# Gate and routing of a gated cross-attention and mixture-of-experts layer: searches in the logits, softmax and tables on GpSimd, more fillers on TensorE

## The reference, cut to what matters

```python
def _L0_ffn_ref(x, gate_w, w1, b1, w2, b2):
    gate_logits = jnp.einsum('bsh,eh->bse', x, gate_w)
    gate_probs = jax.nn.softmax(gate_logits, axis=-1)
    top_v, top_i = jax.lax.top_k(gate_probs, TOP_K)
    onehot = jax.nn.one_hot(top_i, E, dtype=x.dtype)
    comb_w = jnp.einsum('bsk,bske->bse', top_v, onehot)
    out = jnp.zeros_like(x)
    for e in range(E):
        h = jax.nn.silu(jnp.einsum('bsh,hf->bsf', x, w1[e]) + b1[e])
        y = jnp.einsum('bsf,fh->bsh', h, w2[e]) + b2[e]
        out = out + y * comb_w[..., e:e + 1]
    return out
x = x + jnp.tanh(g_xattn[0]) * _L0_xattn_ref(_layernorm(x), ctx_1024, itok, Wq, Wkv, Wo)
x = x + jnp.tanh(g_ffn[0]) * _L0_ffn_ref(_layernorm(x), gate_w, w1, b1, w2, b2)
```

## Time and profile before

| | us |
|---|---|
| runs | 357.92, 358.46, 357.48 (median 357.92) |
| profiled execution, its own time | 356.72 |
| its span, first to last instruction | 355.0 |
| busy: PE / DVE / POOL / ACT | 325.0 / 269.9 / 206.1 / 174.1 |
| mean granted clock of TensorE | 0.976 |

### The profile page before, as it was taken

The page is one execution under the profiler, slowest core; times in us unless marked ns, Lnnn a source line. Parts: engine busy times, 40 slices in busy tenths (PEclk is TensorE's granted clock), DMA queues, the critical chain, the costliest instruction groups (busy, mean ns, idle before and its releaser), DMA issues.

```text
span 355.0 us, 11408 instructions
## 1 busy us (share of the span) xinstructions
PE 325.0 (92%) x3466; PEld 268.6 (76%) x3466; DVE 269.9 (76%) x638; ACT 174.1 (49%) x490; POOL 206.1 (58%) x223
## 2 busy tenths in 40 slices
PE   6798999999989889999999999999999999999930
PEld 6557878888789678888888888888888887778710
DVE  4479999999977987778877788787887875665520
ACT  2451355565464456656465565654656543253400
POOL 3486889996752071566647757467573864662330
PEclk9999999999996999999999999999999999999995
DMA  7699999998999421132323323232332323242210
GB/s 251 201 343 416 408 416 403 416 404 325 347 384 394 113 64 34 32 60 37 52 41 63 46 48 48 47 63 40 55 47 49 51 44 62 36 65 26 35 18 13
DMA packets 31406, 53.23 MB, mean 150 GB/s; under 512 B 4834, under 2 KB 25554, under 8 KB 29300
## 3 DMA queue, kind: packets, MB, share of 16 engines
q0 software_dynamic: 9408, 26.63, 29.3%
q1 hardware_dynamic: 15972, 22.44, 17.4%
q10 hardware_dynamic: 5968, 3.39, 3.2%
HBM read 42.29 MB, written 10.17 MB: 148 GB/s over the span
## 4 chain that ended last, share of the span: by engine, by line
PE 64%; DVE 21%; issue 4%; DMA 4%; ACT 2%; POOL 2%; DVEq 0%; ACTq 0%; POOLq 0%
PE ps L1082 29%; PE ps L1096 16%; PE ps L1099 8%; DVE ps L1262 5%; DVE sel L1258 3%; PE ps L1110 2%; PE ps L1104 2%; DVE w_parts L1258 2%; DMA sel<-near_rows,win_near 2%; DMA tokens_split<-xsplit 1%; DVE xs L1294 1%; PE ps L1103 1%; PE ps L1098 1%; PE ps L837 1%; DVE ps L1266 1%
## 5 line engine op out<-in xcount | busy, mean ns | idle before, releaser
L1082 PE MATMUL ps<-sel,w_parts 128*128 128x128 f16 x1776 | 141.3, 219 | 0.9 <-issue 0.9
L1082 PEld LDWEIGHTS ps<-sel,w_parts 128*128 x1776 | 119.4, 98 | 25.7 <-issue 1.4
L816 ACT ACTIVATE sel<-ps,b1T 128x128 f32<-128x128 f32 x296 | 84.3, 368 | 91.2 <-PE ps L1082 90.7
L589 POOL DMA_INDIRECT out<-sel x37 | 63.2, 1707 | 85.2 <-DVE sel L1532 73.2
L1096 PE MATMUL ps<-w_parts,sel 128*128 x259 | 96.4, 379 | 0.4
L1099 PE MATMUL ps<-w_parts,sel 128*128 x259 | 70.6, 273 | 0.0
L581 POOL DMA_INDIRECT sel<-tokens_split,sel x37 | 45.1, 1219 | 19.2 <-DVE sel L1455 12.7
L1487 DVE SCALAR_TENSOR_TENSOR sel<-sel 128x512 f16<-128x512 f32 x74 | 51.3, 693 | 2.5
L1473 DVE SCALAR_TENSOR_TENSOR w_parts<-w_parts (+1 forms) x32 | 39.0, 1220 | 8.4 <-issue 6.9
L1485 DVE TENSOR_SCALAR sel<-sel 128x512 f16<-128x512 f32 x74 | 33.6, 454 | 9.9 <-ACT sel L816 9.5
L576 POOL TENSOR_TENSOR sel<-sel 128x1 f32<-128x1 f32 x37 | 38.6, 1043 | 1.9 <-PE ps L1110 1.9
(11 more groups left out here) (221 smaller groups left out, 466.6 us busy)
## 6 DMA issues: line engine op xcount, KB each, us to landing
w_parts<-in_L_ffn_w SPq DMA_DIRECT2D x16, 1024.0 KB
out<-xs SPq DMA_DIRECT2D x16, 128.0 KB
tokens_split<-xsplit ACTq DMA_DIRECT2D x16, 128.0 KB, 5.7
xs<-in_x ACTq DMA_DIRECT2D x2, 512.0 KB, 7.0
near_rows<-w_parts SPq DMA_DIRECT2D x4, 256.0 KB, 6.2
xs<-in_x SPq DMA_DIRECT2D x2, 512.0 KB
sel<-tokens_split,sel POOLq DMA_INDIRECT x37
out<-sel POOLq DMA_INDIRECT x37
```

The costliest lines, as they stand in the source:

```text
L589: pool.indirect_dma_start(out_rows, bass.IndirectOffsetOnAxis(slot_row[:, at(q - 1)], 0), y_sb[(k + 3) % 4], None, compute_op=ALU.add).the ...
L816: act.activation(h32[n][:, c * P:c * P + P], ps_h[n][:, c * P:c * P + P], ACT.Silu, bias=biases[:, c:c + 1], scale=1.0 / (X_SCALE * W_SCALE))\
L1082: mm = pe.matmul(ps_h[n][:, c * P:c * P + P], w, xx, start=(i == 0), stop=(i == len(products) - 1))
```

## The change

The two searches run in the logits and no longer in the probabilities, now in a part of 11 tiles and one of 5. The softmax's subtraction goes to POOL, in one instruction for 16 tiles, its exponential is one instruction on ACT, its sum and reciprocal stay on DVE after the running sum, and the weights are multiplied on POOL in three instructions. POOL also takes the experts' order (13 instructions instead of DVE's 3), the small tables (4 instead of 3) and the two products by the token's number. All of these stand in POOL's program behind the last norms; the clearing of `b2_wide` and the gathers stand behind them. PE has more fillers between the last logits (10, 10, 12, 8 where 4, 4, 8, 4 stood) and fewer after them (36 for 48).

```diff
@@ POOL
             norms(T - 1, 1)
+            pool.wait_ge(s["rt"], RT_TOP)
+            pool.tensor_tensor(r_tmp[:, :, :], logit[:, :, :], r_m8[:, :, 0:1].to_broadcast([P, T, E]), ALU.subtract)\
+                .then_inc(s["shifts_ok"], 1)
             remainder(T - 2)
             remainder(T - 1)
+            pool.wait_ge(s["rt_exp"], 1)
+            pool.tensor_scalar(r_p[:, :, :], r_ex[:, :, :], gate2[:, 0:1], None, ALU.mult).then_inc(s["comb_ok"], 1)
+            pool.wait_ge(s["rt"], RT_CUM)
+            pool.wait_ge(s["comb_ok"], 1)
+            pool.tensor_tensor(r_p[:, :, :], r_p[:, :, :], r_m16[:, :, :], ALU.mult).then_inc(s["comb_ok"], 1)
+            pool.wait_ge(s["rt"], RT_INVERSE)
+            pool.wait_ge(s["comb_ok"], 2)
+            pool.tensor_tensor(r_comb[:, :, :], r_p[:, :, :], <r_rs over experts>, ALU.mult).then_inc(s["comb_ok"], 2)
+            pool.wait_ge(s["rt"], RT_RANK)
+            for r in range(E):
+                ins = pool.tensor_scalar(r_by[:, r, :], r_rank[:, :], float(r), None, ALU.is_equal)
+            ins.then_inc(s["ordering"], 1)
...
+            pool.tensor_copy(order_i[:, 1:E + 1], order_f[:, :]).then_inc(s["ordered"], 1)
+            pool.wait_ge(s["span_ok"], 1)
+            pool.tensor_scalar(e_new[:, :], iota[0:E, 0:NT], e_col[:, 0:1], None, ALU.is_equal).then_inc(s["tables"], 1)
+            pool.tensor_scalar(e_ended[:, :], iota[0:E, 0:NT], e_col[:, 1:2], None, ALU.is_ge).then_inc(s["tables"], 1)
+            pool.tensor_scalar(e_own[:, :], iota[0:E, 0:NT], e_col[:, 0:1], None, ALU.is_ge).then_inc(s["tables"], 1)
+            pool.wait_ge(s["tables"], 3)
+            pool.tensor_tensor(e_own[:, :], e_own[:, :], e_ended[:, :], ALU.subtract).then_inc(s["tables"], 1)
+            for h in range(2):
+                tokens = slice(T // 2 * h, T // 2 * h + T // 2)
+                pool.wait_ge(s["rt"], RT_HOT + 1 + h)
+                pool.tensor_tensor(col_tok[:, tokens, :, :], col_tok[:, tokens, :, :], spread_pairs(tok16[:, :], NT),
+                                   ALU.mult).then_inc(s["tok_ok"], 1)
             pool.wait_ge(s["o_ps"], T)
             pool.memset(b2_wide, 0.0).then_inc(s["b2_zeroed"], 1)
@@ ACT
-            act.wait_ge(s["rt"], RT_SHIFT)
-            act.activation(r_ex[:, 0:LATE, :], r_tmp[:, 0:LATE, :], ACT.Exp).then_inc(s["rt_exp"], 1)
...
-            act.wait_ge(s["rt"], RT_SHIFT_LATE)
-            act.activation(r_ex[:, LATE:T, :], r_tmp[:, LATE:T, :], ACT.Exp).then_inc(s["rt_exp"], 1)
+            act.wait_ge(s["shifts_ok"], 1)
+            act.activation(r_ex[:, :, :], r_tmp[:, :, :], ACT.Exp).then_inc(s["rt_exp"], 1)
...
-            act.wait_ge(s["rt"], RT_COMB)
+            act.wait_ge(s["comb_ok"], 4)
...
-            act.wait_ge(s["rt"], RT_ORDER)
+            act.wait_ge(s["ordered"], 1)
@@ PE
             second_turn(T - 3)
-            spin(4)
+            spin(10)
             logits(T - 3)
             second_turn(T - 2)
-            spin(4)
+            spin(10)
             logits(T - 2)
+            spin(12)
+            second_turn(T - 1)
             spin(8)
-            second_turn(T - 1)
-            spin(4)
             logits(T - 1)
-            spin(48)
+            spin(36)
             pe.wait_ge(s["rt"], RT_CUM)
...
             pe.wait_ge(s["rt"], RT_ROWS)
+            pe.wait_ge(s["tok_ok"], 1)
             rows_into_list(0, 8)
...
             pe.wait_ge(s["rt"], RT_ROWS + 2)
+            pe.wait_ge(s["tok_ok"], 2)
             rows_into_list(16, 24)
@@ DVE
-            def shifted_logits(some):
+            def top_two(some):
                 dve.wait_ge(s["logit_ok"], some.stop)
-                link(v.tensor_reduce(r_mx[:, some], logit[:, some, :], AX_X, ALU.max))
-                link(v.tensor_tensor(r_tmp[:, some, :], logit[:, some, :], by_expert(r_mx[:, some]), ALU.subtract))
-            def choose(some, part):
-                dve.wait_ge(s["rt_exp"], part + 1)
-                link(v.tensor_reduce(r_sum[:, some], r_ex[:, some, :], AX_X, ALU.add))
-                link(v.reciprocal(r_rs[:, some], r_sum[:, some]))
-                link(v.tensor_tensor(r_p[:, some, :], r_ex[:, some, :], by_expert(r_rs[:, some]), ALU.mult))
                 for t in range(some.start, some.stop):
-                    ins = v.max(r_m8[:, t, :], r_p[:, t, :])
+                    ins = v.max(r_m8[:, t, :], logit[:, t, :])
                 link(ins)
...
-            shifted_logits(slice(0, LATE))
+            early, late = slice(0, T - 5), slice(T - 5, T)
+            top_two(early)
             residual(T - 1)
             second_moments(T - 1)
-            choose(slice(0, LATE), 0)
-            shifted_logits(slice(LATE, T))
-            choose(slice(LATE, T), 1)
+            chosen(early)
+            top_two(late)
+            assert done[0] == RT_TOP
+            chosen(late)
...
-            link(v.scalar_tensor_tensor(out=r_comb[:, :, :], in0=r_p[:, :, :], scalar=gate2[:, 0:1], in1=r_m16[:, :, :],
-                                        op0=ALU.mult, op1=ALU.mult))
+            dve.wait_ge(s["rt_exp"], 1)
+            link(v.tensor_reduce(r_sum[:, :], r_ex[:, :, :], AX_X, ALU.add))
+            link(v.reciprocal(r_rs[:, :], r_sum[:, :]))
...
-            for h in range(2):
-                dve.wait_ge(s["rt"], RT_HOT + 1 + h)
-                count(v.tensor_tensor(col_tok[:, halves_of[h], :, :], <same>, spread_pairs(tok16[:, :], NT), ALU.mult))
...
-                if first == 8:
-                    dve.wait_ge(s["span_ok"], 1)
-                    <e_ended, e_new, e_own: three instructions>
-            <r_by, r_by, order_i: three links>
...
+            dve.wait_ge(s["ordered"], 1)
             for u in range(2):
                 split_weights(u)
```

More of the change, by code:

```diff
@@ new lines, in _ @@
+            for r in range(E):
+                ins = pool.tensor_scalar(r_by[:, r, :], r_rank[:, :], float(r), None, ALU.is_equal)
+            ins.then_inc(s["ordering"], 1)
+            pool.wait_ge(s["ordering"], 1)
+            pool.tensor_tensor(r_by[:, :, :], r_by[:, :, :], spread_mid(iota[:, 1:E + 1], E), ALU.mult)                .then_inc(s["ordering"], 1)
+            for n in (4, 2):
+                pool.wait_ge(s["ordering"], 4 - n // 2)
+                pool.tensor_tensor(r_by[:, :, 0:n], r_by[:, :, 0:n], r_by[:, :, n:2 * n], ALU.add)                    .then_inc(s["ordering"], 1)
@@ new lines, in _ @@
+            pool.wait_ge(s["ordering"], 4)
+            pool.tensor_tensor(order_f[:, :], r_by[:, :, 0], r_by[:, :, 1], ALU.add).then_inc(s["ordering"], 1)
+            pool.wait_ge(s["ordering"], 5)
+            pool.tensor_copy(order_i[:, 1:E + 1], order_f[:, :]).then_inc(s["ordered"], 1)
+            pool.wait_ge(s["span_ok"], 1)
+            pool.tensor_scalar(e_new[:, :], iota[0:E, 0:NT], e_col[:, 0:1], None, ALU.is_equal).then_inc(s["tables"], 1)
+            pool.tensor_scalar(e_ended[:, :], iota[0:E, 0:NT], e_col[:, 1:2], None, ALU.is_ge).then_inc(s["tables"], 1)
@@ L1328, in _, with chosen @@
             experts = iota[:, 0:E]
[L1330 removed]
+            def top_two(some):
                 dve.wait_ge(s["logit_ok"], some.stop)
[L1333 to L1342 removed]
                 for t in range(some.start, some.stop):
[L1344 removed]
+                    ins = v.max(r_m8[:, t, :], logit[:, t, :])
                 link(ins)
                 for t in range(some.start, some.stop):
[L1347 removed]
+                    ins = v.max_index(r_i8[:, t, :], r_m8[:, t, :], logit[:, t, :])
                 link(ins)
+            def chosen(some):
+                n = some.stop - some.start
                 link(v.tensor_copy(r_i2[:, some, :], r_i8[:, some, 0:2]))
@@ L1379, in _ @@
             link(v.tensor_reduce(r_rank[:, :], r_more[:, :, :], AX_X, ALU.add))
+            assert done[0] == RT_RANK
             link(v.tensor_tensor(r_more[:, :, :], r_more[:, :, :], spread_mid(r_tf[:, :], E), ALU.mult))
@@ L1427, in _ @@
                     assert done[0] == RT_ROWS
-                if first == 8:
-                    dve.wait_ge(s["span_ok"], 1)
[L1430 to L1434, removed]
-            ranks = iota[:, 0:E].rearrange("p (r o) -> p r o", o=1).to_broadcast([P, E, E])
-            link(v.tensor_tensor(r_by[:, :, :], spread_mid(r_rank[:, :], E), ranks, ALU.is_equal))
-            link(v.tensor_tensor(r_by[:, :, :], r_by[:, :, :], spread_mid(iota[:, 1:E + 1], E), ALU.mult))
-            with nc.allow_low_precision(reason="one small whole number and zeros"):
-                link(v.tensor_reduce(order_i[:, 1:E + 1], r_by[:, :, :], AX_X, ALU.add))
-            assert done[0] == RT_ORDER
             dve.wait_ge(s["tile_ok"], 1)
```

22 lines of the change are left out of this document (11 added, 11 removed).

## The result

| | before | changed |
|---|---|---|
| median of 8 runs, us | 358.28 | 360.76 |
| lowest and highest, us | 357.48, 358.76 | 358.71, 362.74 |
| profiled execution, own time / span, us | 356.72 / 355.0 | 358.71 / 357.0 |
| ratio | | 1.0076, 95% interval 1.0051 to 1.0100 |

The change makes the kernel slower by 0.76%, about 2.7 us (1.8 to 3.6); the two medians lie 2.5 us apart. Forecast was +1.3 us, 359.2 with a range of its own of 358.0 to 360.3. The median of 360.76 lies above that range and inside the wider one of 355.9 to 361.6. The profiled execution is the fastest of the changed kernel's eight and lies 2.0 us over that of before. The last comparison made, that of the kernel with only the token products on POOL, also holds four executions in a slower state (391 us; 362, 388 and 480 us for the kernel before), and all ratios here leave such executions out.

The account below looks back on a forecast made before the run. PE bounds the experts' stage, so only its start moves, through the DVE chain before it: -0.7 - 1.3 + 0.8 + 2.3 = +1.1, plus 0.2 for the clock, +1.3 on 357.92: 359.2 us, own range 358.0 to 360.3, wider 355.9 to 361.6.

Parts of the forecast that it names:

- What bounds, and what the change is worth: Experts' stage: PE sets the pace, untouched; the change is worth the shift at the list's first instruction, carried unchanged to the end.
- part 4: From r_row to the list: tables, order and token products on POOL take 7.5 us for 5.2, +2.3.
- part 3: POOL and DVE beside each other up to r_row: each waits for the other's running two-input SBUF instruction, +0.8 us.
- rival 2: Drain: the clock falls all the same, +0.8 us instead of -0.7, so 360.7 us; chance 0.17.
- Part 1: Drain up to the last logits: added fillers hold PE's clock, -0.7 us, ends -0.7 and +0.8.
- Part 2: Last logits to running sum: DVE needs 2.2 us for 3.62, -1.4; sum and reciprocal behind add 0.1; together -1.3 us.
- the rule: Trainium skill on SBUF: a two-input VectorE instruction and a GpSimd one reading SBUF contend; the second waits for the whole other.
- The sign to look for: Profile after, r_row to list: DVE idle before the list, POOL's order instructions spread to 0.5 us each during row_hot.
- The sign against me: Forecast wrong if DVE's last row_hot piece is not later than r_row + 3.4 us.
- Free running: Rival: POOL and DVE run side by side without waits, list at 120.7, -1.6 us, 356.3; chance 0.26, with cheap products.
- PE starving: Rival: PE waits before the list, clock drops, 72 fillers delay the experts' first transpose; about +1, 360.2 us; chance 0.19.
- the 0.2 us allowed for it: Behind the list: allowance for the 72 fillers running partly at the low clock after PE idles some 3 us.

## Why the prediction was right, and where its sizes were off

- **What bounds, and what the change is worth.** Right: from the list on all is shifted; the last stretch of the table changed by 0.08 us, and the experts' stage, 0.3 us shorter, is within the 226.9 to 227.4 us that it takes in all but one of the profiled executions here.
- **The size.** Too small. The chain of the profiled execution grew by 2.24 us for 1.3; of the 0.9 us between them part 4 makes up 0.8, and the waits of part 3 0.3, less 0.2 elsewhere. The runs rose by 2.5 to 2.7 us. By its number the median, 360.76, lies at rival 2's 360.7 and not in the forecast's own range; the profiled execution shows the forecast's mechanism, with the clock at 1.00. No trace of the other seven says which case they were.
- **Part 1, the drain.** Right in mechanism and size (-0.74 against -0.7) in the profiled execution. Which case comes is not settled by the fillers alone: over the changed kernel and the experiments rival 2, at 1.3 to 1.5 us, came in three of eight profiled executions. I gave it 0.17, which looks too little. It may be a part of why the runs rose by more than the profiled execution (2.7 for 2.0 us); that is not shown.
- **Part 2, searches and softmax.** Right: with the halves moved the searches' stretch is 2.43 us, and without what is left of waits in the pair and the members (0.24 and 0.04 over the 0.30 and 0.29 that they should take alone, an estimate from the rows for four and twelve tiles) 2.2 us, as worked out; the sum and reciprocal cost 0.13 for 0.1.
- **Part 3, waits.** Right in mechanism, 1.1 for 0.8 us in size, and at another place than I spread them. All of it lies in the one-hot pair and the members, behind the subtraction and the two `remainder`. In the chain from the counts to `r_row`, where I had put four short waits, none was lost: 3.63 us for 3.60, while POOL did its eight 0.27 us comparisons. So the sentence that the rule "denies that the moved work lies beside DVE's at all" went too far: beside this chain of short instructions, reductions among them, the comparisons cost nothing.
- **Part 4, the term that was mis-sized.** +3.1 for +2.3, that is 8.4 us for 7.5. Its pieces: DVE's run 3.5 us for 3.3, products 2.4 for 2.5, order and tables outside the run 1.3 for 0.9, and from the end of the products to the list 1.2 for 0.8 (123.40 to 124.57). The last is in part the clock, which is at 0.50 from 123 on: the two groups of list matmuls take 0.43 and 0.47 us where 0.37 stood. The products were worked out at 1.27 us and took 1.20. Order and tables were set at 0.9 us out of 0 to 2.5; they took until 121.0, 1.3 us behind the end of DVE's run at 119.7. Two causes of that: POOL's small comparisons cost 0.27 and 0.39 us and not the 0.19 of the smallest row, and from the 64-element product to the end of the tables they took 1.9 us more than with one of DVE's inputs in PSUM (4.8 for 2.9). The sign to look for, DVE idle in front of the list and POOL's instructions at about 0.5 us each during `row_hot`, was there. The products came after DVE's run, so they did not hold it up. So it was luck that the sum of run and products, 5.8 us, came out (5.9): it was founded on their taking turns, but DVE's run was hardly stretched, and the products simply stood at the end. The sign against me, a last `row_hot` piece not later than `r_row` + 3.4 us, told little: the piece ended 3.5 us behind `r_row`, and without any wait it would have been 3.3.
- **Rivals.** Free running is denied by the operands in PSUM and by the products alone on POOL. PE starving is denied by the first transpose, which comes as soon behind the list as before, and the halved fillers gained nothing. The low clock lengthened the two groups of list matmuls by 0.16 us together and moved the ten fillers by at most 0.1 us more, so the 0.2 us allowed for it were about right.

## What to carry to other kernels

In these runs work moved from DVE to POOL lay beside DVE's while DVE did searches and reductions or took one operand from PSUM. Against a run of two-input products it was added to the sum: two long products of POOL held DVE's run up by 2.06 us. Count the small instructions too: short operations on POOL that met DVE's run took up to 0.95 us longer. Eight of them beside a chain of short DVE instructions, a few with two inputs, cost 0.03 us. Sort POOL's queue so that its products fall on DVE's reductions and searches. And take a change apart before judging it: here a part that gained and one that lost more were in one.

## What the runs showed of the hardware that I had not expected

- The same small POOL instructions (order and tables) took 0.19 to 0.40 us each beside DVE's run with one operand in PSUM, and 0.32 to 1.35 us each beside the run with both in SBUF (the changed kernel and the one with the token products on DVE).
- A product of DVE with a float16 operand in SBUF and a float32 one in PSUM takes 1.15 us for 1024 elements (4.61/4) where both in SBUF as float16 take 0.64 (2.56/4).
- TensorE's granted clock did not fall while PE waited for POOL (1.00 from 119.1 to 122), but once it had gone on with the list (0.98 from 122 to 123, 0.50 from 123 to 126).
- The start of the drain (logit matmuls of tile 13) varied from 103.66 to 105.36 us over the ten profiled executions, in large part by what ACT waits for the transfer of an earlier token tile: 0.7 of the 1.3 us between these two (103.97 and 105.24). Waits of ACT from 95 to 112, us in total, times, longest; first the changed kernel, then the one with the fillers alone:

```profile
ACT xsplit L718 <- DMA tokens_split<-xsplit: 0.3, 1, 0.3
```

```profile
ACT xsplit L675 <- DMA tokens_split<-xsplit: 1.0, 1, 1.0
```

The spread of 3 to 4 us over the runs of each kernel, the one before too (356.07 to 359.88 over 30), may come from this and from the clock's two cases; no run was made that holds one of them fixed. But the runs on record narrow it down. In the eight kernels with the changed fillers the standard deviation of the runs is 1.0 to 1.4 us, also where nothing else was changed (1.1); with the fillers of before it is 0.4 to 0.9, also with the changed routing (0.76). So the wider part of the spread came with the fillers. That the clock makes it, at its higher level in one execution and at its lower in another, fits this and is not shown.
